# Attention and mixture-of-experts block: the attention stage's order of work on five engines is rewritten around the score phases

## What is computed

```
x = x + tanh(g_xattn) * attention(layernorm(x), ctx)
x = x + tanh(g_ffn)   * experts(layernorm(x))

attention(x, xa):            # 16 heads of width 8
    q, k, v    = heads(x @ Wqkv + bqkv)
    _, ka, va  = heads(xa @ Wqkv_aux + bqkv_aux)
    p  = softmax(q k^T / sqrt(8));  pa = softmax(q ka^T / sqrt(8))
    out = (p v) * (1 - sigmoid(g)) + (pa va) * sigmoid(g)
    return out @ Wo + bo

experts(x):                  # 64 experts of width 64, 8 chosen per token out of 4 of 8 groups, and a shared one
    y = sum_e w_e(x) * (silu(x @ Wg_e) * (x @ Wu_e)) @ Wd_e
```

## Time and profile before

| | |
|---|---|
| median of 3 runs | 874.07 us (872.4 to 875.69) |
| span of the profiled execution | 867.8 us, with 6.3 us around it to the median |
| PE, PEld busy | 834.5 us (96%), 647.4 us (75%) |
| DVE, ACT, POOL busy | 692.7 us (80%), 566.3 us (65%), 637.0 us (73%) |
| attention stage | from the start to about 299 us |
| expert stage | the rest |

### The profile page before, as it was taken

How to read it: one execution, slowest core, us unless ns; L and a number is a source line. 1 busy time by engine, 2 the same in 40 slices (tenths; PEclk the granted TensorE clock), 3 DMA queues, 4 the chain that set the end, 5 groups by cost and what they waited for, 6 DMA issues and landing times.

```text
span 867.8 us, 20170 instructions
## 1 busy us (share of the span) xinstructions
PE 834.5 (96%) x6733; PEld 647.4 (75%) x6733; DVE 692.7 (80%) x1656; ACT 566.3 (65%) x964; POOL 637.0 (73%) x602
## 2 busy tenths in 40 slices
PE   5899999999998899999999999999999999999997
PEld 3466777776765677888888888877888888888885
DVE  6888999998988769778777887967966977876655
ACT  4378788887877756576576566548557556656554
POOL 2577888888863358787786787877877778778785
PEclk9999999999999999999999999999999999999999
DMA  5677677677653066566554654744755654656552
GB/s 133 181 182 183 177 206 185 185 198 185 160 161 92 24 155 142 132 144 146 121 142 118 160 132 120 172 127 102 180 126 135 146 139 122 152 128 147 139 133 62
DMA packets 113746, 125.26 MB, mean 144 GB/s; under 512 B 28000, under 2 KB 76064, under 8 KB 112208
## 3 DMA queue, kind: packets, MB, share of 16 engines
q1 hardware_dynamic: 110768, 123.47, 57.0%
q10 hardware_dynamic: 2880, 0.59, 0.4%
HBM read 103.55 MB, written 19.96 MB: 142 GB/s over the span
## 4 chain that ended last, share of the span: by engine, by line
PE 67%; DMA 5%; DVE 3%; issue 1%; ACT 1%; POOL 1%; SPq 0%; DVEq 0%; POOLq 0%; ACTq 0%
PE bank L1964 20%; PE bank L1966 19%; PE bank L1965 19%; DMA stack_k<-k_scratch 2%; PE bank L1305 2%; DMA cwb<-wts_scratch 1%; PE bank L1292 1%; PE bank L1279 1%; DMA stack_q<-nmaxT 1%; PE bank L1261 1%; DMA x_scratch<-x 1%; PE bank L1941 1%; ACT prob L787 0%; DVE mx L984 0%; DVE hlo L1876 0%
## 5 line engine op out<-in xcount | busy, mean ns | idle before, releaser
L1641 POOL TENSOR_TENSOR hid<-act,cwb 128x512 f32<-128x512 f32 x264 | 423.7, 1614 | 127.6 <-DVE act L1868 74.7
L1694 ACT ACTIVATE silu<-bank 128x512 f32<-128x512 f32 x256 | 152.7, 597 | 190.7 <-PE bank L1966 186.2
L1868 DVE TENSOR_TENSOR act<-silu,bank 128x512 f32<-128x512 f32 (+1 forms) x264 | 180.2, 682 | 116.8 <-ACT silu L1694 76.6
L1876 DVE TENSOR_TENSOR hlo<-hid,hhi 128x512 fp32r<-128x512 f32 x256 | 201.0, 786 | 9.0 <-ACT hhi L1700 8.7
L1964 PE MATMUL bank<-xhi,weights_hi 128*128 128x512 f32 x520 | 206.8, 398 | 1.1 <-ACT silu L1694 1.1
L1966 PE MATMUL bank<-xlo,weights_hi 128*128 128x512 f32 x520 | 204.2, 393 | 0.0
L1965 PE MATMUL bank<-xhi,weights_lo 128*128 128x512 f32 x520 | 204.0, 392 | 0.0
L984 DVE TENSOR_REDUCE mx<-bank 128x4 f32<-128x512 f32 x256 | 167.3, 685 | 15.3 <-PE bank L1279 11.1
L1700 ACT ACTIVATE hhi<-hid 128x512 fp32r<-128x512 f32 (+1 forms) x264 | 165.0, 626 | 17.0 <-POOL hid L1641 15.4
L787 ACT ACTIVATE prob<-bank 128x1024 f32<-128x1024 f32 x128 | 131.0, 1024 | 59.0 <-PE bank L1292 56.4
L1964 PEld LDWEIGHTS bank<-xhi,weights_hi 128*128 128x128 f32 x520 | 97.6, 188 | 22.9 <-ACT silu L1694 2.1
(11 more groups left out here) (235 smaller groups left out, 1003.2 us busy)
## 6 DMA issues: line engine op xcount, KB each, us to landing
cwb<-wts_scratch SPq DMA_DIRECT2D x174, 384.0 KB, 5.4
stack_k<-k_scratch SPq DMA_DIRECT2D x30, 384.0 KB
k_scratch<-parts_k SPq DMA_DIRECT2D x15, 384.0 KB, 3.3
stack_q<-q_scratch SPq DMA_DIRECT2D x30, 192.0 KB
k_scratch<-parts_k SPq DMA_DIRECT2D x15, 256.0 KB, 3.7
q_scratch<-parts_q SPq DMA_DIRECT2D x15, 192.0 KB, 2.3
xin<-in_x_dram SPq DMA_DIRECT2D x16, 128.0 KB, 2.6
cin<-in_ctx_dram SPq DMA_DIRECT2D x16, 128.0 KB, 2.5
```

The lines of the kernel that those rows point to most:

```text
L1641: pool.tensor_tensor(h_buf[k][:], a_buf[k][:], cwb[slot][:, q % GP, :], ALU.mult).then_inc(h_ok, 1)
L1694: act.activation(s_buf[k % RS][:], g_bank[k % 2][:], ACT.Silu).then_inc(s_ok, 1)
L1868: nc.vector.tensor_tensor(a_buf[k % RS][at], s_buf[k % RS][at], u_bank[k % 3][at], ALU.mult).then_inc(a_ok, 1)
L1876: nc.vector.tensor_tensor(hlo[k % RH][:], h_buf[k % RS][:], hhi[k % RH][:].bitcast(F32), ALU.subtract).then_inc(hl_ok, 1)
```

## The change

It rewrites the order of the attention stage on PE, DVE and ACT, and what this order needs.

- **Sums of two rounds together.** `weighted` stands only after phase 1 (round 3 of b-1 and round 0 of b) and after phase 3 (rounds 1 and 2 of b). RP is 3, so that the exponentials of three rounds are held.
- **Full-array work in two slots.** After phase 0: `turn_att` b-2, `project_v` or `project_qk`, `turn_max` b+1. After phase 2: `out_proj` b-2, `transposes` or `project_ka`, `turn_o` b-1. Turning back, projection and residual of a batch come one batch later than before.
- **Scores two batches ahead, one maximum a round.** The scores run 8 units in front (all of b+2 in batch b), in the order of heads 8, 10, 12, 14, 0, 2, 4, 6. `maxima` takes both banks in one instruction (128x1024) and adds 2 to its semaphore.
- **V in 18 columns.** The tile is VS = 18 columns a head; the sums still stand 32 columns apart, so the `o_bank` tiles are cleared once at the start on DVE.
- The ACT queue issues `shift_rows` after round 0's work and ahead of the exponential of round 1. `high_of` of an odd batch moves from round 0 to round 3, and POOL takes its rest a chunk later. On DVE `minus_max` stands at the start of a batch, `evac_nmax` after the maximum of round 0, and `residual`, `copy_ka` and `normalise` all after the maximum of round 2.

```
-S_HEAD = (10, 12, 14, 0, 2, 4, 6, 8)
+S_HEAD = (8, 10, 12, 14, 0, 2, 4, 6)
 VW = 32
-RP = 2
-LAG = 2
-AHEAD = 7
+VS = 18
+RP = 3
...
-        def maxima(b, par, u):
-            wait(dve, s_mm, UNITS * b + u + 1)
-            if u == 0:
+        def maxima(b, par, r):
+            u = 2 * r
+            wait(dve, s_mm, UNITS * b + u + 2)
+            if r == 0:
                 wait(dve, nm_ok, b - 1)
             f, h = S_HEAD[u] // HH, S_HEAD[u] % HH
-            nc.vector.tensor_reduce(mx[par][:, 2 * f:2 * f + 2, h:h + 2].rearrange("p a h -> p h a"),
-                                    s_bank[u % 2][:].rearrange("p (h a k) -> p h a k", h=2, a=2),
-                                    AXX, ALU.max).then_inc(mx_ok, 1)
+            nc.vector.tensor_reduce(mx[par][:, 2 * f:2 * f + 2, h:h + 4].rearrange("p a h -> p h a"),
+                                    s_wide[:].rearrange("p (h a k) -> p h a k", h=4, a=2),
+                                    AXX, ALU.max).then_inc(mx_ok, 2)
...
+                score_phase(b, 0)
+                if b > 1:
+                    turn_att(b - 2, odd)
+                if not odd and more:
...
+                    project_v(n + 1, (i + 1) % 2, 0)
+                    project_v(n + 1, (i + 1) % 2, 1)
+                if odd and ahead:
+                    wait(pe, v_ev, n + 2)
+                    project_qk(n + 3, 1 - i)
...
+                if b < NB - 1:
+                    wait(pe, nm_ev, b + 1)
+                    turn_max(b + 1)
+
+                score_phase(b, 1)
+                if b > 0:
+                    for u in (UNITS - 2, UNITS - 1):
+                        weighted(b - 1, 1 - odd, u, (b - 1) // CH, (b - 1) // CH % 2)
+                for u in (0, 1):
+                    weighted(b, odd, u, n, i)
+
+                score_phase(b, 2)
+                if b > 1:
+                    out_proj(b - 2, odd)
...
+                if not odd and ahead:
+                    wait(pe, nm_ev, b + 2)
+                    transposes(n + 3, 1 - i)
+                if odd and ahead:
+                    project_ka(n + 3, 1 - i)
...
+                if b > 0:
+                    turn_o(b - 1, 1 - odd)
+
+                score_phase(b, 3)
+                for u in range(2, UNITS - 2):
+                    weighted(b, odd, u, n, i)
```

More of the change, by code:

```diff
@@ L914, in on_dve @@
     def on_dve(dve):
+        for par in range(2):
+            nc.vector.memset(o_bank[par][:], 0.0)
         nc.vector.memset(nmax[:], 0.0)
@@ new lines, in body @@
+                if one_more:
+                    if b == NB - 2:
+                        dve.wait_ge(fe_ok, 1)
+                    minus_max(b + 1, 1 - odd, min(n + 3 + odd, NC))
+                if two_more:
+                    maxima(b + 2, odd, 0)
+                if one_more:
+                    evac_nmax(b + 1)
+                if first:
+                    norm_sums(3)
+                    norm_mean(3)
+                if not odd and n + 4 < NC:
+                    norm_sums(n + 4)
@@ new lines, in body @@
+                stats_and_route(left, k, 0)
+                if two_more:
+                    maxima(b + 2, odd, 1)
+                if not odd and n + 4 < NC:
+                    norm_mean(n + 4)
+                stats_and_route(left, k, 1)
+                if two_more:
+                    maxima(b + 2, odd, 2)
+                if first:
+                    bias_row()
+                if b > 1:
+                    residual_of(b - 2)
+                if odd and n + 3 < NC:
+                    copy_ka(n + 3)
@@ L1229, in on_dve @@
+                if not first:
+                    normalise(b - 1, 1 - odd)
+                stats_and_route(left, k, 2)
+                if two_more:
+                    maxima(b + 2, odd, 3)
+                stats_and_route(left, k, 3)
+            if last:
+                residual_of(NB - 2)
         for g in range(LOOPS - 2):
@@ L1387, in on_pe @@
         turn_max(0)
-        for u in range(AHEAD):
+        for u in range(UNITS):
             scores(1, u, 0)
@@ new lines, in body @@
+                ahead = n + 3 < NC
+                score_phase(b, 0)
+                if b > 1:
+                    turn_att(b - 2, odd)
+                if not odd and more:
+                    if last:
+                        pe.wait_ge(fg_ev, 1)
+                    wait(pe, ka_ev, min(n + 3, NC))
+                    project_v(n + 1, (i + 1) % 2, 0)
[3 more added lines that the diff above has]
+                    project_qk(n + 3, 1 - i)
```

268 lines of the change are left out of this document (109 added, 159 removed).

## The result

The changed kernel takes 898.97 us (median of 4 runs, 897.75 to 904.11) beside 874.88 (872.4 to 877.52) for the kernel before: a ratio of 1.029, 95% interval 1.026 to 1.032, slower by 24 us. The forecast was 888 us, its range ended at 896. The direction was right, the size too small by 11 us.

What follows compares the result with a forecast made beforehand. PE was taken as the bound in attention, DVE close behind. Pairs lengthened from 16.46 to 17.2 us add 9.6 us and the start 4: 874 + 9.6 + 4 = 887.7, say 888 us, range 869 to 896.

Steps and rivals of the forecast that it cites:

- The steady pair: Two attention batches: 14.7 us on PE plus holds after phases 3 and 1, 17.15, taken as 17.2 against 16.46 before.
- behind phase 3: `normalise` and the joined maximum delay the next phase's scores to 2.09 us and full-array work to 2.62: 0.47 extra a batch.
- The slot after phase 2: PE work of `weighted`-free slot with `out_proj`, transposes or `project_ka`, and `turn_o`, phase start to phase start: 2.25 us.
- After phase 1: DMA issue of turned maxima, plus rounding in even batches, delays round 1's exponential: 0.54 us extra odd, 0.96 even.
- It supposes that the pairs that were late before are late no more: Attention loop: the 8 us of late pairs disappear, as POOL waits less and longer pairs give stacks more time.
- The third rival: Slower still: late pairs stay late, with POOL or the DMA behind; 8 us more, 893 to 896 us; chance 0.14.
- Before the loop: Prologue scores of batches 0 and 1: eight joined rounds of 1.9 to 2.2 us; 4 us more, bounds 2 and 6.5.
- Tail: Batches 30 and 31, without scores: only the exponential loop; costs within 1 us either way.
- V in 18 columns, the third `prob`, clearing at nothing: Narrower V tiles, a third held exponential tile and clearing `o_bank` at the start were each counted as no time.
- Fewer switches: Tile-kind changes on PE fall from 12 to 8 a batch, at about 0.11 us each: 0.9 us saved a pair.
- 14.7 on PE alone: Time in us of a pair of batches if PE's own work alone set the pace, summed from four slots a batch.
- The first rival: The switches decide: PE alone sets the pair at 14.7 us or waits stay hidden; 856 us; chance 0.12.

Runs made afterwards that it cites:

- e8: Changed kernel with only the rounding of the weights behind the exponential of round 1, the DMA of the turned maxima staying ahead: 898.66 us, ratio 1.026.
- e1: Changed kernel with the DMA of the turned maxima and the rounding both behind the exponential of round 1: 896.86 us, ratio 1.029.
- e6: Kernel before, with only `shift_rows` (DMA of the turned maxima) moved ahead of the exponential of round 1: 880.91 us, ratio 1.010.
- e12: e7 with the DMA of the turned maxima ahead of the exponential of round 1 again, the rounding behind it: 877.46 us, ratio 1.003.
- e3: Changed kernel with `norm_sums` one round later on DVE, behind the maximum of round 1: 891.41 us, ratio 1.022.
- e9: Changed kernel with the store of a chunk's x one chunk later on SP, behind the loads: 896.56 us, ratio 1.026.
- e4: Changed kernel with one maximum a bank in the prologue only (batches 0 and 1): 896.46 us, ratio 1.026.
- e2: Changed kernel with one maximum a bank again in the loop only, the prologue keeping the joined one: 896.05 us, ratio 1.029.
- e5: Changed kernel with the edits of e1, e2, e3 and e4 together: 873.64 us, ratio 0.999.
- e7: e5 with the later store of x of e9: 872.42 us, ratio 0.998.
- e15: e7 with one more wait on SP, issuing a chunk's stack_k loads only once the odd batch's turned maxima are copied: 869.38 us, ratio 0.9945.

## Why the prediction was right or wrong

*The steady pair: right in its mechanism, and closer in its size than its terms are.* 17.27 against 17.15 worked out and 17.2 taken. Most steps hold: the joined maximum 1.22 (1.21 said); phase 1 to 2 2.52 in the even batch (1.60 + 0.96 = 2.56 said), 2.16 in the odd (2.14 said); behind phase 3 of the even batch the scores 2.20 (2.09 said), full-array work 2.73 (2.62 said). Two steps don't, and that they cancel is luck. Behind phase 3 of the odd batch full-array work comes at 3.06, 0.44 later than said, since the step left `copy_ka` on DVE out. The slot after phase 2 takes 2.14 and 2.06, where 2.25 was said, 0.30 a pair less. Over 14 pairs the steady pair makes 11.4 of the 20.1 us, and the sum had 9.6.

*After phase 1: right in sum, wrong in its halves.* I took 0.54 of each batch as the DMA's. e8 and e1 show 0.36 a pair for the rounding (0.42 said) and only 0.07 for the DMA. The step's own bounds had 0.31 a batch left by the maximum loop once the hold goes. In e1 that much is left from phase to phase, and the joined maximum then keeps back the scores of phase 2 besides. e6 and e12 show the full price of the DMA, 0.7 to 0.8 a pair, where the maxima are apart.

*"It supposes that the pairs that were late before are late no more": this step failed, and it carries most of the miss.* 250.5 less 14 x 17.27 = 241.8 leaves 8.7 us of late pairs, where I let the 8 of before disappear and put nothing in their place. They are mostly new: three pairs (22.10, 18.68, 17.99) hold 7.0 of the 8.7. I read POOL and the stacks as what was late, and let a longer pair cure them. I didn't see that `norm_sums` in its new place asks for the context 3.2 us sooner in its pair, with the maximum of round 1 and so PE behind it; and I didn't follow SP past the residual that comes one batch later (69.1 us of waits against 26.3), with the store of q and `load_x` behind it. With `norm_sums` one round later (e3) 2.3 of the 8.7 us are left, with the store of x later (e9) 5.8. The third rival came nearest in size (893 to 896), but for the DMA share and POOL.

*Before the loop: mis-sized.* 6.7 us, not 4, just over the bound of 6.5. The joined maxima of the prologue start 2.4 to 2.5 us apart (DVE's timeline: 23.55, 25.97, 28.45, 30.87), where I had 1.9 to 2.2; from the round's first score (24.83) to its maximum (25.97) it is 1.14 us, where I had added up at most 0.95. The credit for batch 1 running beside a DMA was not there. e4 shows the maxima as the cause, 6.3 of 6.7. The clock is not it, though it looks so: from 20 to 40 us the granted clock is 0.50 in the changed kernel's trace and 1.00 in that of before. But it is 1.00 there in e2 and e8 too, and their first `project_v` of the loop still comes at 43.65 and 43.67; and it is 0.50 there in e6, which has it at 36.98.

*Tail: 2.2 us, not within 1.* 1.3 us lie between the last `project_v` and the first matmul of the experts (267.42 to 299.21 before, 294.37 to 327.45 after), and 0.9 in the expert stage, which the change leaves alone. The expert stage takes 568.6 to 574.4 us in the traces here, so the 0.9 shows nothing. No run looked into the 1.3. *V in 18 columns, the third `prob`, clearing at nothing*: nothing in the traces speaks against it, and none was tried alone.

*Fewer switches.* e5's pair of 15.53 is below 15.88, so the new order has a gain in it; my 14.7 on PE alone was not reached in any run. The first rival (856 us) took the gain as the whole.

Beside the steps: 2.7 (start) + 1.8 (steady pairs) + 8.7 (late ones) + 2.2 (tail) is 15.4 us on the spans; the medians lie 5.0 closer than the spans, which leaves 10.4 of the 11.

## What to carry to other kernels

A step moved one batch later moves everything that waits for it: follow it into each DMA queue, and ask what is queued behind the waiting store or load. And a step moved up, as `norm_sums` here, asks for its data sooner: compare its place with that of the load, and ask what stands behind it on its engine. Two maxima of one bank each are worth more than one over both where a producer fills one bank while the other is read: joining saved 0.07 us of work and cost 0.7 to 1.3 us a pair. And single edits price a hold only as far as the next hold: here four gave 15 us apart and 25 together by the medians, 20.6 and 26.0 by the start of the last `project_v`, so a part of a change that looks free in one place (the DMA issue, 0.07) can cost ten times as much in another.

## What was not expected of the hardware

After PE had stood for 2.34 us inside the phase at 83.17 us, following waits of 0.66 and 0.25, its granted clock was 0.74 from 84 to 86 us, 0.50 (the 1.2 GHz level) from 86 to 90 and 0.55 from 90 to 92, while PE was busy all of the last six. The pair is 4.8 us late. The stall is 2.3 of them; the rest is about what six us at a mean clock of 0.52 (4 at 0.50, 2 at 0.55) lose, an estimate of 2.9, if PE alone set the pace there. In e3, where the stall is gone, the granted clock stays at 1.00.

In e7 a small DMA of turned maxima (16 KB), issued 2.6 us behind stack loads of 768 KB, kept PE waiting 0.86 us at 202.26, although its issue (196.59) lay 5.7 us ahead of that phase. At 89.09 PE waited 2.1 us for the one issued at 82.18, 1.0 us behind the stack loads. With the stack loads held back, so that the two are issued side by side (0.4 us apart at 191.51, e15), PE waited at most 0.9 us in the whole run. I had costed the place of a small DMA by its issue alone.
